# Front of a Mamba and memory block: x is loaded behind the store of u's first half, and the second batch's statistics open the next chunk

## The reference

```python
g = _gn(x)                      # group norm, 32 groups, over (16 channels x 64 x 64)
xn = (xf - mu) * rsqrt(var + EPS) * ln_w + ln_b      # per token, over 512 channels
xin, z = split(xn @ in_proj_w.T)                     # 1024 + 1024 columns
u = silu(causal_conv1d(xin, taps=4) + conv_b)
x_dbl = u @ x_proj_w.T                               # 32 (dt) + 16 (B) + 16 (C)
delta = softplus(x_dbl[:, :32] @ dt_proj_w.T + dt_proj_b)
y = selective_scan(u, delta, A, B, C, D) * silu(z)
x = x + y @ out_proj_w.T
```

## Time and profile before

| | us |
|---|---|
| median of 3 runs | 4791.86 (4790.72 to 4792.37) |
| profiled execution, its time | 4792.53 |
| its span | 4790.7 |
| front, about | 50 to 1110 |
| TensorE busy | 4464.4 (93%) |
| VectorE busy | 3960.8 (83%) |
| ScalarE busy | 2812.4 (59%) |
| GpSimd busy | 2813.2 (59%) |

### The profile page before, as it was taken

The page is one execution under the profiler, slowest core; times in us unless marked ns, Lnnn a source line. Parts: engine busy times, 40 slices in busy tenths (PEclk is TensorE's granted clock), DMA queues, the critical chain, the costliest instruction groups (busy, mean ns, idle before and its releaser), DMA issues. The chain is left out here.

```text
span 4790.7 us, 110599 instructions
## 1 busy us (share of the span) xinstructions
PE 4464.4 (93%) x47036; PEld 2961.1 (62%) x47036; DVE 3960.8 (83%) x4161; ACT 2812.4 (59%) x5941; POOL 2813.2 (59%) x1257
## 2 busy tenths in 40 slices
PE   6888888896899999999999999999998899999999
PEld 5566666664555555555555555555554787887887
DVE  6666766667999999999999999999997777777332
ACT  2444555555777777777777777777765444443211
POOL 0111111115999999999999999999996222222000
PEclk9899999998999999999999999999999999999999
DMA  4444444345323332333233323332332121121553
GB/s 157 145 156 176 146 159 150 143 164 160 90 79 99 99 100 81 99 99 99 83 100 101 101 83 101 99 99 80 100 99 74 62 80 58 75 80 79 202 202 141
DMA packets 195257, 538.60 MB, mean 112 GB/s; under 512 B 15600, under 2 KB 15616, under 8 KB 185680
## 3 DMA queue, kind: packets, MB, share of 16 engines
q1 hardware_dynamic: 189888, 482.41, 30.5%
q0 software_dynamic: 4880, 49.12, 2.6%
HBM read 329.09 MB, written 202.38 MB: 111 GB/s over the span
## 5 line engine op out<-in xcount | busy, mean ns | idle before, releaser
L992 POOL TENSOR_TENSOR sc_hc<-sc_hc,sc_c_rep 128x1024 f32<-128x1024 f32 x1024 | 2388.0, 2375 | 129.3 <-ACT sc_state L1005 99.9
L1187 DVE TENSOR_TENSOR_SCAN sc_hc<-l_m,sc_state,sc_ring 128x512 f32<-128x512 f32 x2048 | 2421.5, 1268 | 11.3 <-PE sc_y_ps L1124 5.7
L1037 ACT ACTIVATE l_m<-l1s_v,l_neg_a 128x512 f32<-128x512 f32 x2048 | 1351.6, 707 | 12.0 <-DMA l1s_v<-spill 11.9
L1114 PEld LDWEIGHTS sc_ring<-sc_diag,l1s_iota 64*64 64x64 f32 x32768 | 898.6, 133 | 458.5 <-issue 452.6
L1114 PE MATMUL sc_ring<-sc_diag,l1s_iota 64*64 64x128 f32 x32768 | 1043.1, 274 | 45.0 <-DVE sc_hc L1187 41.7
L1124 PE MATMUL sc_y_ps<-sc_hc,sc_fold 128*64 128x512 f32 x4096 | 936.0, 599 | 0.9 <-POOL sc_hc L992 0.9
L379 POOL TENSOR_TENSOR fr_du<-fr_u,fr_delta 128x1024 f32<-128x1024 f32 x60 | 142.9, 2404 | 923.7 <-ACT fr_delta L437 923.7
L1005 ACT ACTIVATE sc_state<-sc_hc 128x2 f32<-128x2 f32 x1024 | 207.0, 202 | 622.1 <-DVE sc_hc L1187 621.6
L1124 PEld LDWEIGHTS sc_y_ps<-sc_hc,sc_fold 128*64 128x64 f32 x4096 | 271.5, 136 | 484.8 <-issue 461.9
L1456 POOL TENSOR_TENSOR l_count<-l_count,as_oh 128x1024 f32<-128x1024 f32 x64 | 183.8, 2872 | 523.4 <-DVE as_oh L1652 523.4
L875 PE MATMUL sc_o_ps<-l_et,l_sums 128*128 128x512 f32 x960 | 464.0, 606 | 4.4 <-ACT sc_b_col L1015 4.4
(11 more groups left out here) (185 smaller groups left out, 5375.4 us busy)
## 6 DMA issues: line engine op xcount, KB each, us to landing
sc_duz<-spill SPq DMA_DIRECT2D x128, 768.0 KB, 6.0
l1s_v<-spill SPq DMA_DIRECT2D x256, 256.0 KB, 4.1
spill<-fr_z SPq DMA_DIRECT2D x64, 512.0 KB, 2.8
spill<-fr_u SPq DMA_DIRECT2D x32, 1024.0 KB, 5.9
spill<-fr_delta SPq DMA_DIRECT2D x32, 1024.0 KB, 5.2
spill<-fr_du SPq DMA_DIRECT2D x32, 1024.0 KB, 6.6
sc_c_rep<-bc SPq DMA_DIRECT2D x128, 256.0 KB, 4.4
soft<-l_et SPq DMA_DIRECT2D x16, 2048.0 KB, 6.2
```

What stands on the lines that cost most here:

```text
L992: nc.gpsimd.tensor_tensor(hc[:, p], hc[:, p], c_rep[:, 2 * q:2 * q + 2, :], ALU.mult).then_inc(s_hp, 1)
L1037: nc.scalar.activation(da[:, p % 4, r, :], delta[:, i % 2, p % 2, :], ACT.Exp, scale=keep.neg_a[:, c:c + 1]).then_inc(s_da, 1)
L1114: done = nc.tensor.matmul(to[:, :, k::4], dut[rows, i % 2, k, HALF * h:HALF * h + HALF], diag[rows, u, 4 * q + c:4 * q + 4:2, k, :], start ...
L1187: nc.vector.tensor_tensor_scan(hc[:, p, r, :], da[:, p % 4, r, :], ring[:, SLOT[at], r::2], state[:, i, 2 * p + r:2 * p + r + 1], ALU.mult ...
```

## The change

The load of x: chunk 1's stays ahead of the loop; the others, `load(g + 2)`, are issued in chunk g behind `store_u(g, 0)` and ahead of `store_z(g, 2)`. It waits for `split(g + 1)`, which is in chunk g too. In chunk 0 the wait for the first four `bn_stats` and the second load for the statistics go behind `store_z(0, 2)`. The statistics of chunk g (1 to 7) are computed at the beginning of chunk g, ahead of `norm_v` or `group_means`, and no longer behind conv 5 of chunk g - 1. The first ones, `next_batch(0)`, stay.

```diff
@@ -338,9 +338,8 @@
             def load_next_batch(j):
                 sp.dma_start(sq[:], x_view[1, j]).then_inc(s_xs, 16)
 
+            load(1)
             for g in range(NG):
-                if g + 1 < NG:
-                    load(g + 1)
                 if g:
                     store_bc(g - 1)
                 store_z(g, 0)
@@ -353,10 +352,12 @@
                     store_delta(g - 1, 1)
                 store_z(g, 1)
                 store_u(g, 0)
+                if g + 2 < NG:
+                    load(g + 2)
+                store_z(g, 2)
                 if g == 0:
                     sp.wait_ge(s_bn, KC)
                     load_next_batch(1)
-                store_z(g, 2)
                 store_z(g, 3)
                 store_u(g, 1)
             store_bc(NG - 1)
@@ -728,6 +729,8 @@
             split(0)
             for g in range(NG):
                 more = g + 1 < NG
+                if 0 < g < NJ:
+                    next_batch(g)
                 if turns(g):
                     group_means()
                 elif more:
@@ -769,8 +772,6 @@
                 if g == 0:
                     next_batch(0)
                 conv(g, 5)
-                if g + 1 < NJ:
-                    next_batch(g + 1)
                 conv(g, 6)
                 conv(g, 7)
             add_halves(NG - 1)
```

## The result

The changed kernel takes 4645.88 us in the median (4643.44 to 4647.30, 4 runs) beside 4791.29 for the kernel before: a ratio of 0.9696, 95% interval 0.9679 to 0.9713, 145 us less. The forecast was 4650, range 4632 to 4683. The profiled execution has a span of 4645.5 us and took 4647.3. The lines of the changed kernel are numbered up to one higher (L621 is L622, L678 is L679).

A forecast was written before the change was run, and what follows sets the result against it. Waits bound the front: each chunk VectorE waits for the load of x, then TensorE for xd. Gains of 14.0, 55.5, 1.3, 10.5, 61.0 and 0.2 us make 142.5, so 4792.5 - 142.5 = 4650 us, range 4632 to 4683.

The forecast's parts named there:

- the clock: TensorE's granted clock at chunk starts, taken as 1.00; if it falls, 1.6 us a chunk, 21 us in 13.
- the 13 waits: VectorE's waits before `norm_v` for the load of x, opening chunks 1 to 6 and 8 to 14: 137.8 us.
- Part 1: Load of x lands 8.7 us after split at the latest, against 9.3 or 11.8; residue costed at nothing.
- Part 2: Four `bn_stats`, 2.4 to 2.5 us, move to the next chunk's front: nothing added, chunk 0's 2.70 us wait goes.
- The walk through a chunk: Step-by-step timing of a new chunk: 55.0 us in chunks 2 to 6, 53.4 us in chunks 8 to 13.
- T: End of a chunk's last convolution, from which the next chunk's steps are timed; 335.72 in the trace.
- The wait for the root: VectorE's wait for ScalarE's root ahead of the reciprocal, forecast to stay at 6.9 us.
- TensorE's own work: TensorE's work without a wait, 53.6 us a chunk, which set the low end of the range.
- (a): Rival: the load of x lands late at its new place, 31 us back, 4681 us; chance 0.10.
- (b): Rival: GpSimd's products meet `norm_v` and its add, 4.1 us in 13 chunks, 53 back, 4703 us; chance 0.04.
- (c): Rival: xd is held by something else, for instance SyncE stuck at a store, 4792 us; chance 0.02.
- (d): Rival: SyncE's wait for `split` delays z's stores, stopping ScalarE; 4804 us at 21 us late; chance 0.01.

The follow-up runs named there:

- E7: Kernel before the change, with z block 0 projected four times in the chunks whose `mean` waits for xd: 4784.97 us, 0.9987.
- E1: Changed kernel with the load of x moved but the statistics put back behind convolution 5: 4663.69 us, 0.9729.
- E3: Changed kernel with an extra 1 MB load of the same x into a spare tile ahead of each load from chunk 2's on: 4648.66 us, 0.9698.
- E8: E3 with a second extra 1 MB transfer, memory to memory, ahead of each real load of x from chunk 2's on: 4660.53 us, 0.9730.
- E4: Kernel before the change, with z block 0 projected three times in the chunks whose `mean` waits for xd: 4802.64 us, 1.0021.
- E5: Changed kernel with ScalarE's root for the next chunk ahead of silu of z block 2 and of softplus: 4619.89 us, 0.9642.
- E6: Changed kernel where in chunk 7 GpSimd's first product waits for VectorE's `add_values(8)`: 4636.49 us, 0.9677.

## Why the prediction was right

**What bounds the kernel.** Right: the load's wait was on the path, nearly one for one. 137.8 us of it and 2.7 in chunk 0 make 140.5, and the front gained 146.4. E7, with its 6.5 us, makes the clock the likely rest. By stretches the match is looser: 53.1 us of waits gave 57.2 in chunks 1 to 5, where the clock's gain comes on top, and 62.8 gave 60.4 in chunks 8 to 13, where TensorE is late next, as forecast. In E1 the 13 waits are gone as well and the front gains 129.2 us; the rest needs the statistics' move.

**Part 1, the load's cover.** Right, and with more room than said: it lands 5.7 to 6.4 us behind its issue (5.9 in the median) instead of up to 8.5, with half a MB issued beside it and not one. Against 9.3 and 11.8 nothing is left to wait for. (The prediction's 8.7 us "at the latest" is 0.4 and the median of 8.3; with the 8.5 at most it is 8.9, and the cover 0.4 and not 0.6.) E3 and E8 show the cover's edge between 9.2 us and 10.6 us of landing in the chunks without statistics.

**Part 2, the statistics.** Right that the move adds nothing: a chunk with statistics takes 1.4 us more than one without (54.67 and 53.2), as forecast. The prediction left open what the old place would have cost beside the early load. E1: 18 us, 1.8 a chunk in chunks 1 to 5, and 3.6 and 3.7 in chunks 0 and 6.

**The walk through a chunk.** Forecast from T: xd 6.3, var 20.0, reciprocal 30.4, end 55.0. Measured: 6.2, 19.7, 30.1, 54.7. Without statistics: 53.4 against 53.2, but for chunk 8, which follows the turn and took 54.8. The wait for the root stayed, at 7.07.

**The clock.** Right that it stays at 1.00 at the chunk starts, but for that of chunk 8: there TensorE waits 2.02 us for the last u again, and the clock is 0.57 behind it. In chunk 4 that wait is down from 2.02 to 0.89 us, which goes with the reason given, x_proj's last pair no longer being waited for. But it is only part of it: in chunk 5 of the kernel before, and in chunk 4 of E4, the same wait was there and the clock stayed. The start of chunk 4, where the earlier trace rows had 0.50, and that of chunk 8:

```profile
296.00:298.00 2.00, 2.00 (x7) 1.01 (x8) 2.00 (x5) 1.03 (x2) 0.00 (x0) 1.00 0.33 125
...
525.13 1.07 PE L560 MATMUL fr_st_ps<-fr_u,l0f_w_xp 128*64 128x512 f32 x2 [2.02 <-ACT fr_u L422]
526.00:528.00 2.00, 2.00 (x6) 1.50 (x6) 1.93 (x3) 0.59 (x1) 0.00 (x0) 0.57 0.73 265
```

**What was mis-sized.** TensorE's own work, 53.6 us a chunk, came out of a sum of matmul durations and of five projections of 2.7 us; E5 has 52.24. x_proj was put at 4.7 us and takes 3.65 where u is there in time, and `var` is counted twice, as the 32.1 us start with it and the 3.1 hold it again; against that stand 0.7 us of waiting for `var`. The forecast of the chunks without statistics came within 0.2 us all the same, since the chain through VectorE and ScalarE set them. And in E4's expectation the xd-to-var stretch of one chunk was taken for all. The 4 us by which the front gained more than forecast lie in small pieces, 1.2 us up to chunk 1, 1.7 in chunks 1 to 5 and 1.3 in chunk 7; which term was short in each isn't shown.

**The rivals.** (a) needs 1 to 2 MB more traffic (E3, E8). (b) exists in chunk 7 alone, before and after (`norm_v` 4.00 us at 471.55, 1.9 in all other chunks). (c) is excluded by the row of the load at 285.96. (d): SyncE waits 109.6 us in 13 times for the split, and no engine's waits name a store of z in the changed kernel; its threshold of 20 us wasn't tried.

## What to carry to other kernels

A queue's order is part of the schedule: a load that has been free to go for some 14 us (split over at 324.0, issue at 337.87) but stands behind a store can be worth its whole flight time in each round (10.5 us here), and the place for it is right behind the last reader's end. Other work near the boundary goes to the side where the engine that is late next doesn't wait for it. Which engine that is can be told by walking one round of the trace, taking each stretch from several rounds and not from one, and timing an operation where nothing holds it back. And a wait of 7 us a round that stands on the chain gives back only what the next engine's own work leaves: 26 of 92 us here.

## What the runs showed of the hardware

- Transfers of 1 MB issued close together did not simply follow each other: 5.9 us to landing beside half a MB, 9.2 us behind another load of 1 MB issued 0.4 us earlier (E3), 10.6 behind two, one of them memory to memory (E8).
- TensorE's granted clock fell from 2.4 to 1.2 GHz behind 2.0 us of idling in x_proj at the start of chunk 4 of the kernel before, and did not fall behind the same 2.0 us at the start of chunk 5 (matmuls again at 403.12, clock 1.00 from 404 to 412) nor in chunk 4 of E4. What tells them apart stays open. Filling a wait in part moved the fall to a dearer place: 11 us slower than not filling it (E4).
- VectorE's `norm_v` and add took 4.00 and 3.25 us beside GpSimd's product and 1.92 and 1.23 without it (E6). The Trainium skill (SBUF — State Buffer, "Who interferes with whom") says that VectorE operations in a two-port mode, or with two inputs in SBUF, and a GpSimd operation that reads SBUF lock each other out for a whole instruction; the trace agrees in that both operations took about 2 us longer, and doesn't show in which mode `norm_v` ran.
